# TensorE's first-pass work issued in parts: scores, head products and exponents cut up, with gate products, counts and turns between the parts

## The reference

```python
x = x + tanh(g_xattn[0]) * mlstm(layernorm(x), ctx, ctx, ...)      # gated linear attention, 4 heads of 32
x = x + tanh(g_ffn[0])   * moe(layernorm(x), wg, w1, b1, w2, b2)   # top-1 of 8 experts, with capacity
x = x + tanh(g_xattn[1]) * attention(layernorm(x), ctx, ctx, mask) # softmax attention, projected q and k
x = x + tanh(g_ffn[1])   * (layernorm(x) @ CB.T * SCB / 127 + bias)

def mlstm_head(q, k, v, ig, fg):          # ig, fg: input and forget gate of each token, from q, k, v
    cs = cumsum(log_sigmoid(fg))
    log_d = where(lower_triangle, cs_i - cs_j + ig_j, -inf)
    m = max(log_d, axis=-1)
    c = q @ k.T / sqrt(dh) * exp(log_d - m)
    n = maximum(sum(c), exp(-m))
    return c / (n + eps) @ v
```

## Time and profile before

| | |
|---|---|
| time, median of 3 runs | 593.76 us (592.67 to 594.1) |
| the profiled execution's own time | 595.22 us |
| its span, first to last instruction | 593.5 us |
| PE busy over the span | 483.4 us (81%), mean granted clock 0.843 |
| the first pass | from the start to about 300 us of the span |
| steps with all of stages one to three | about 49 to 258 us |

### The profile page before, as it was taken

How to read it: one execution, slowest core, us unless ns; L and a number is a source line. 1 busy time by engine, 2 the same in 40 slices (tenths; PEclk the granted TensorE clock), 3 DMA queues, 4 the chain that set the end, 5 groups by cost and what they waited for, 6 DMA issues and landing times. The chain is left out here.

```text
span 593.5 us, 12772 instructions
## 1 busy us (share of the span) xinstructions
PE 483.4 (81%) x3787; PEld 360.7 (61%) x3787; DVE 334.0 (56%) x1455; ACT 307.1 (52%) x764; POOL 217.3 (37%) x210
## 2 busy tenths in 40 slices
PE   0359999999999999984549999999924779888884
PEld 0346778788787877863425777777722456666652
DVE  6223578877787877678423222222213577777872
ACT  1346676656566656531203333333403678888872
POOL 5200114444434444546520000000048888888400
PEclk9998777867677767787558999999975898999997
DMA  5971112222222211140120433443142456666521
GB/s 137 189 165 56 55 56 68 79 72 69 71 67 71 73 54 49 46 120 30 33 70 24 107 107 106 106 106 107 36 119 36 101 98 143 141 142 141 128 88 38
DMA packets 85067, 51.98 MB, mean 88 GB/s; under 512 B 7555, under 2 KB 78886, under 8 KB 85030
## 3 DMA queue, kind: packets, MB, share of 16 engines
q1 hardware_dynamic: 73766, 43.09, 27.0%
q0 software_dynamic: 11264, 8.43, 8.2%
HBM read 26.07 MB, written 16.91 MB: 72 GB/s over the span
## 5 line engine op out<-in xcount | busy, mean ns | idle before, releaser
L666 POOL DMA_INDIRECT s_xs<-slots_y,s_gidx x64 | 98.9, 1545 | 154.4 <-DMA slots_y<-s_ye 135.2
L795 ACT ACTIVATE s_ht<-heads,s_cols 128x512 f32<-128x512 f32 x64 | 44.0, 687 | 85.5 <-PE heads L1036 85.2
L147 ACT ACTIVATE s_xn<-s_xs,s_ln_shift,s_ln_rstd 128x128 f32 (+1 forms) x192 | 77.6, 481 | 16.7 <-DVE s_ln_shift L140 16.6
L99 DVE BATCH_NORM_STATS2 s_ln_stats<-s_xs 128x6 f32 (+1 forms) x256 | 54.7, 279 | 35.3 <-DMA s_xs<-slots_y,s_gidx 20.9
L644 POOL DMA_INDIRECT slots_x<-s_xn,s_sidx x64 | 62.9, 983 | 22.9 <-issue 22.9
L1036 PE MATMUL heads<-s_xet,s_w_sb 128*128 128x512 f32 x128 | 60.6, 618 | 1.7 <-DVE s_xet L1396 1.7
L630 POOL TENSOR_TENSOR s_hs<-s_hs,s_head_w 128x512 f32<-128x512 f32 x16 | 20.3, 1269 | 111.5 <-DVE s_hs L1280 111.5
L1043 PE MATMUL bank<-s_w_sb,s_ht 128*128 128x128 f32 x512 | 59.9, 275 | 0.9 <-DVE s_ye L1405 0.9
L1043 PEld LDWEIGHTS bank<-s_w_sb,s_ht 128*128 128x128 f32 x512 | 58.5, 192 | 1.5 <-issue 1.5
L935 PE MATMUL heads<-s_dec_r,s_dec_l 128*128 128x512 f32 x64 | 52.5, 970 | 0.0
L960 PE MATMUL heads<-s_vaug,s_cw 64*64 64x33 f32 x1024 | 49.3, 267 | 0.1
(11 more groups left out here) (190 smaller groups left out, 946.9 us busy)
## 6 DMA issues: line engine op xcount, KB each, us to landing
slots_x<-s_xe SPq DMA_DIRECT2D x8, 516.0 KB, 11.3
s_xe<-slots_x SPq DMA_DIRECT2D x16, 258.0 KB, 3.1
s_xs<-in_x_dram SPq DMA_DIRECT2D x16, 256.0 KB, 2.9
s_ctxb<-in_ctx_dram SPq DMA_DIRECT2D x16, 256.0 KB, 3.2
s_kpt<-s_kt SPq DMA_DIRECT2D x16, 256.0 KB, 2.4
s_w_sb<-in_L_ffn_w_dram SPq DMA_DIRECT2D x16, 256.0 KB, 3.2
slots_y<-s_ye SPq DMA_DIRECT2D x16, 256.0 KB, 2.3
s_ctxv<-in_ctx_dram SPq DMA_DIRECT2D x16, 256.0 KB, 3.5
```

Source lines behind the costliest of these rows:

```text
L99: last = dve.bn_stats(self.stats[:, i * GT + t, :], tile(t))
L147: last = act.activation(out(t), tile(t), ACT.Identity, bias=self.shift[:, j:j + 1], scale=self.rstd[:, j:j + 1])
L666: pool.indirect_dma_start(out=xs[:, n * D:(n + 1) * D], out_offset=None, in_=slots_y, in_offset=bass.IndirectOffsetOnAxis(ap=gidx[:, n:n + ...
L795: act.activation(ht[:, s_par, c, :], heads[:, c, :], ACT.Gelu_apprx_tanh, bias=col).then_inc(h_done, 1)
```

## The change

PE's step is written in another order, and four of its functions take the tiles or the half that they are to issue:

- `scores` is issued as tiles 0 and 1, then `turn_maxima`, then tiles 2 and 3.
- `gate_products` and `head_values` are interleaved: gate tiles 0 and 1, head tile 0, gate tile 2, head tile 1, gate tile 3, head tile 2. Then comes `turn_routed`, and head tile 3 behind it.
- `decay_exponents` is issued as its first product, then `forget_sums` and `turn_queries`, then its second product, then `turn_context`. The semaphore `l_ps` now counts twice a group; `decays` on ACT still waits for both products, and SP's `spread_max` still waits for the same group (its count is written for two). The second product waits for the second half of the decayed scores only, the first for the first half.

No product, copy or transfer is added or removed. The diff, with its unchanged surroundings cut:

```diff
@@ -467,7 +467,7 @@
             def spread_max(g, half, q):
 
                 hold(sp, mrow_done, g + 1, consts)
-                hold(sp, l_ps, g - 1, consts)
+                hold(sp, l_ps, nth(g - 2, 2, 2), consts)
                 for b in range(2):
                     sp.dma_start(dec_r[32 + b:33 + b, q, :], mrow[:, q, b * S:(b + 1) * S]).then_inc(m_in[q], 16)
 
@@ -719,7 +719,7 @@
                 act.activation(em[:, q, :], bank[6][:, 256:256 + R], ACT.Exp, scale=-1.0).then_inc(em_done, 1)
 
             def decays(g, half, q):
-                act.wait_ge(l_ps, g + 1)
+                act.wait_ge(l_ps, nth(g, 2, 2))
                 need(act, cw_done, nth(g - 2, 1, 2))
                 act.activation(ex[:, q, :], heads[:, 0:2, :].rearrange("p u n -> p (u n)"), ACT.Exp).then_inc(ex_done, 1)
 
@@ -899,18 +899,20 @@
                     last = pe.transpose(bank[0][:, t * P:(t + 1) * P], xn1[:, t, :], ident[:, :])
                 last.then_inc(xt1_done, 1)
 
-            def gate_products(g, half, q):
-
-                if isinstance(g, int) and g == 0:
-                    pe.wait_ge(dve_setup, 1)
-                pe.wait_ge(kt_done, g + 1)
-                hold(pe, em_done, g, consts)
-                pe.wait_ge(qt_done, g + 1)
-                for t in range(GT):
+            def gate_products(g, q, tiles_of):
+
+                if 0 in tiles_of:
+                    if isinstance(g, int) and g == 0:
+                        pe.wait_ge(dve_setup, 1)
+                    pe.wait_ge(kt_done, g + 1)
+                    hold(pe, em_done, g, consts)
+                    pe.wait_ge(qt_done, g + 1)
+                for t in tiles_of:
                     tile = bank[6][:, t * 2 * NH:(t + 1) * 2 * NH]
                     pe.matmul(tile, kt[:, q, t * P:(t + 1) * P], kc[:, :], start=True, stop=False)
                     last = pe.matmul(tile, qt[:, t * P:(t + 1) * P], kqkv[:, 0, :], start=False, stop=True)
-                last.then_inc(gates_ps, 1)
+                if GT - 1 in tiles_of:
+                    last.then_inc(gates_ps, 1)
 
             def forget_sums(g, half, q):
 
@@ -926,18 +928,17 @@
                 pe.matmul(bank[6][:, 256:256 + R], tri[:, :], logf[:, :], start=True, stop=False)
                 pe.matmul(bank[6][:, 256:256 + R], mrow[:, q, :], ident[0:R, 0:R], start=False, stop=True).then_inc(mt_ps, 1)
 
-            def decay_exponents(g, half, q):
-
-                pe.wait_ge(arow_done, g + 1)
-                hold(pe, m_in[q], half * 32 + 32, consts)
-                need(pe, cw_done, nth(g - 1, 2, 2))
-                for u in range(2):
-                    last = pe.matmul(heads[:, u, :], dec_l[:, q, :], dec_r[:, q, u * GW:(u + 1) * GW], start=True, stop=True)
-                last.then_inc(l_ps, 1)
-
-            def scores(g, half, q):
-
-                for t in range(GT):
+            def decay_exponents(g, half, q, u):
+
+                if u == 0:
+                    pe.wait_ge(arow_done, g + 1)
+                    hold(pe, m_in[q], half * 32 + 32, consts)
+                need(pe, cw_done, nth(g - 1, u + 1, 2))
+                pe.matmul(heads[:, u, :], dec_l[:, q, :], dec_r[:, q, u * GW:(u + 1) * GW], start=True, stop=True).then_inc(l_ps, 1)
+
+            def scores(g, q, tiles_of):
+
+                for t in tiles_of:
                     if t == 0:
                         pe.wait_ge(qbd_done, nth(g, NH, NH))
                         pe.wait_ge(ex_done, g + 1)
@@ -946,9 +947,9 @@
                                          qbd[:, q, b * NH * S:(b + 1) * NH * S], start=True, stop=True)
                     last.then_inc(scores_done, 1)
 
-            def head_values(g, half, q):
-
-                for t in range(GT):
+            def head_values(g, q, tiles_of):
+
+                for t in tiles_of:
                     if t % 2 == 0:
                         hold(pe, cw_done, nth(g, t // 2 + 1, 2), consts)
                     if t == 0:
@@ -995,23 +996,38 @@
             def first_pass(at):
                 zero, one, two, three, _, five, six = at
                 if three:
-                    scores(*three)
+                    scores(three[0], three[2], (0, 1))
                 if two:
                     turn_maxima(*two)
+                if three:
+                    scores(three[0], three[2], (2, 3))
                 if six:
                     count_tokens(*six)
                 if one:
-                    gate_products(*one)
+                    gate_products(one[0], one[2], (0, 1))
                 if three:
-                    head_values(*three)
+                    head_values(three[0], three[2], (0,))
+                if one:
+                    gate_products(one[0], one[2], (2,))
+                if three:
+                    head_values(three[0], three[2], (1,))
+                if one:
+                    gate_products(one[0], one[2], (3,))
+                if three:
+                    head_values(three[0], three[2], (2,))
                 if five:
                     turn_routed(*five)
+                if three:
+                    head_values(three[0], three[2], (3,))
                 if two:
-                    decay_exponents(*two)
+                    decay_exponents(*two, 0)
                 if one:
                     forget_sums(*one)
                 if zero:
                     turn_queries(*zero)
+                if two:
+                    decay_exponents(*two, 1)
+                if zero:
                     turn_context(*zero)
                 if one:
                     turn_a(*one)
@@ -1228,7 +1244,7 @@
 
             def running_max(g, half, q):
                 dve.wait_ge(at_ps, g + 1)
-                need(dve, l_ps, g - 1)
+                need(dve, l_ps, nth(g - 2, 2, 2))
                 dve.tensor_copy(dec_l[0:R, q, :], bank[6][0:R, 128:256]).then_inc(arow_done, 1)
                 if not isinstance(g, int) or g >= 2:
                     dve.wait_ge(m_in[q], half * 32)
```

## The result

The changed kernel takes 625.08 us (median of 4 runs, 623.72 to 626.57) against 593.93 us; the ratio is 1.052, with a 95% interval from 1.048 to 1.056. It is 31 us slower. The forecast had the direction, but 602.8 us for the time and 613 us as the upper end of the range.

What follows compares the result with a forecast made beforehand. PE was taken as the first pass's bound, busy 193.76 of 198 us from 60 to 258 us. Terms 7.2 - 3.9 + 1.7 + 2 + 2 = +9.0 us on the median 593.76 gave 602.8 us, range 587 to 613.

Steps and rivals of the forecast that it cites:

- (a): Between last score and gates, PE waits 1.03 us for keys and `exp_m`, no longer covered by maxima: +7.2 us.
- (b): PE's waits for the running maxima and the one-hot rows ahead of the counts go: -3.9 us.
- (c): The second exponent product ends later, delaying scores in three steps without logits, 0.61 us each: +1.7 us.
- (d): Seven more borders between parts a step, up to 0.08 us each (7.7 us in all): taken as +2 us.
- (e): PE's clock falls and rises once a step as before, low part slightly longer: +2 us, bounds about 11 either way.
- the clock gets worse: Rival, chance 0.12: wide work cut by fourth head tile and forget sums, clock rises later: about 615 to 622 us.
- A clock that falls in a busy engine: In the first pass PE was not idle when its clock fell, so the skill's idle rule does not describe the trace.

Runs made afterwards that it cites:

- E: Kernel before with only the two exponent products apart, forget sums and turned queries between them: 581.9 us, ratio 0.984.
- H: Kernel before with only gates and heads interleaved and the routed transposes ahead of the last head tile: 617.8 us, ratio 1.042.
- S: Kernel before with only the scores in two halves around the transposed maxima: 619.0 us, ratio 1.041.
- filled form: Kernel before plus 16 bf16 products of 240 columns a step that nothing reads: 569.9 us, ratio 0.961.
- S with the fill: Kernel before with scores in two halves around the maxima, plus 16 unread products of 240 columns a step: 590.3 us, ratio 0.984.

## Why the prediction was wrong

**(a) The keys' wait: right.** 1.03 us between the last score and the gates was forecast, 1.04 us is in the timeline, and the list shows 6.1 us of waiting in 12 steps, in the forecast window of 5 to 8.

**(b) The old waits: they went, for the reason given, but were worth less.** The changed kernel has none for the maxima or the one-hot rows. The runs without E show that it hangs on E: without the exponent product in between PE stands idle 6.7 us for the maxima. The term of 3.9 us added the 1.4 us of the weight load to PE's own 1.6 and 0.9 us; weight loads overlap the matmuls, and PE's own idle time for both was 2.5 us.

**(c) The late exponent: right in size.** 1.3 us of waiting for `s_ex`, in 2 of the 3 early steps. The list ends at 258 us; another 0.3 us comes in the step at 286 us, which the forecast did not have.

**(d) The borders: mis-sized.** Forecast 2 us. Of the 11.4 us of full-clock time that were added, 4.5 us are PE's idle time (10.4 against 5.9 us); some 7 us remain for the borders by subtraction, against 6 us (0.45 x 14) for heads and transposes read at full clock. The price of a border, 0.08 us, was about right (0.09). What failed is the discount from 7.7 to 2 us, on the argument that the 0.08 us holds a semaphore wait: the new borders have few waits and cost as much.

**(e) The clock: the step that failed.** The forecast had one fall and one rise in a step "as before, the low part slightly longer: +2 us", with 11 us as the bound, and a mean clock of 0.73 to 0.75 in the steady steps. The fall and the rise are there, as in the step shown; the clock was 0.71, and the size was 12.9 us. What the forecast missed is that the low part does not grow slightly: it came to last 10 us in 12 of 15 steps (17.1 us a step, over and over), where the kernel before has, by its own timeline of `decays`, steps of 14.3 us with 7 us at half clock between those of 16.8 with 10. The forecast's price of such a step was right, 1.6 us for 3.4 us more at half clock (1.7); it did not expect nearly every step to pay it.

The time left the range because (d) and (e) both came out at or beyond their upper ends. Even with both ends the sum gives 593.8 + 23.7 = 617.5 us. Of what is still missing, some 2 us are the terms (a) to (d), read mostly at full clock and paid at a clock of 0.76 (12.7 against 15.0 us), 2 us the part of (e) beyond its bound, 0.6 us lie outside the stretch, and the medians lie 2.7 us further apart than the profiled executions.

The runs show that H takes the clock away: H alone 0.72, whole heads with S and E 0.80; that E gives clock: 0.81 alone; and that S alone has 0.73. The rival "the clock gets worse" (0.12, 615 to 622 us) comes nearest to the measured time, and half of its mechanism holds. It named two cuts in the wide work. The one by the fourth head tile costs 9 us (617.8 us for H alone against 608.5 without the moved transposes). The one by the forget sums is E, and gained 10 us alone and 11 beside S and H. The interleaving of gates and heads, which costs the most, it did not name; the forecast counted it as a long narrow run that stays.

What no run here tells is which property of H lowers the clock. The interleaving without the moved transposes has 16 of its 25 us, so it is not the cut between transposes and exponents alone. That gates and heads in alternation spread the narrow work over a longer time is the likely reading, and was not tested by itself.

**A clock that falls in a busy engine: right.** PE was busy 1.00 of each microsecond around the fall before and is so at 205 to 207 us in the changed kernel, in the windows above; filling the step with wide products held 2.4 GHz (0.97 to 1.00), where being busy with narrow ones did not. (In that step of the changed kernel PE had also been idle for 0.41 us shortly before the fall; the kernel before had not.) Idle time does not decide it: PE is idle 5.9 us of the stretch in the kernel before and in its filled form alike, at 0.76 and at 0.97, and S with the fill is idle 19.6 us and keeps 0.97. The Trainium skill, "TensorE: Matmul & The Clock Gate", section "Why this matters for your kernels", asks, against throughput drops in mid-kernel, for no idle gaps between bursts of matmuls; this trace does not agree that it is enough.

## What to carry to other kernels

Where TensorE is the bound and its clock moves between two levels in every step, read the granted clock times the length of a stretch of equal work first: it splits a difference into work and clock, and two orders of the same instructions differed here by 10 us and more in the second. Parts do not add: S cost 27 us alone and 13 us or less beside E, and E gained 10 us alone and 24 us beside S (595.1 against 619.0); test a part in both companies. If the clock falls while the engine is busy with narrow products, wide products that nothing reads are worth a try: they can pay for themselves; here 16 a step made the kernel 22 us faster, and splitting the exponents (10 us) asked for no extra work at all.

## What the runs showed of the hardware that was not expected

The granted clock fell in a busy engine and stayed up when 3840 more columns a step were streamed (16 x 240): from 0.76 to 0.97 on the kernel before and 1.00 with the exponents apart. With the same products 8 columns wide it was 0.77. With H the same fill gave only 0.85. A group of 16 small products on 64 rows costs 0.59 us between other kinds of product and 0.50 us in a row, at full clock; at half clock 1.00 and 0.89: about 0.1 us at both levels.
